# Attention on Trainium2: eight GpSimd row copies per batch, one behind each of eight heads

## The reference, cut to what matters

```
q, k, v = heads(h @ Wq + bq), heads(h @ Wk + bk), heads(h @ Wv + bv)     # [16, 16, 512, 16]
scores  = q k^T + rel_q + rel_k          # rel_*: products with the table of distances
probs   = softmax(scores / sqrt(16))
ctx     = probs v
```

## Time and profile before

| | us |
|---|---|
| median of three runs | 3165.08 |
| the profiled execution's own time | 3169.93 |
| its span, first to last instruction | 3168.1 |
| busy over the whole span: TensorE matmuls | 2673.8 |
| busy: VectorE | 2019.4 |
| busy: ScalarE | 1617.7 |
| busy: GpSimd | 1785.3 |

### The profile page before, as it was taken

The page is one execution under the profiler, slowest core; times in us unless marked ns, Lnnn a source line. Parts: engine busy times, 40 slices in busy tenths (PEclk is TensorE's granted clock), DMA queues, the critical chain, the costliest instruction groups (busy, mean ns, idle before and its releaser), DMA issues. The chain is left out here.

```text
span 3168.1 us, 51305 instructions
## 1 busy us (share of the span) xinstructions
PE 2673.8 (84%) x18316; PEld 1921.7 (61%) x18316; DVE 2019.4 (64%) x5579; ACT 1617.7 (51%) x2037; POOL 1785.3 (56%) x1486
## 2 busy tenths in 40 slices
PE   4676287978988888858999999999999959999998
PEld 2344187877877878755666666666666635554454
DVE  4665255655755666645666666666666658888885
ACT  2343164545544555526777777777777712222221
POOL 2333123333233233228888889988888825655555
PEclk7888667677776777768999999999999979999999
DMA  3999979999999999999999999999999532222110
GB/s 98 222 216 218 187 267 336 365 329 369 361 355 360 349 353 358 342 326 314 286 292 288 288 294 300 289 279 294 294 292 306 184 138 77 70 92 76 70 51 22
DMA packets 499917, 792.66 MB, mean 250 GB/s; under 512 B 236568, under 2 KB 266592, under 8 KB 465616
## 3 DMA queue, kind: packets, MB, share of 16 engines
q1 hardware_dynamic: 440528, 647.27, 61.4%
q10 hardware_dynamic: 46592, 100.68, 13.7%
q0 software_dynamic: 12544, 41.43, 4.5%
HBM read 449.17 MB, written 340.05 MB: 249 GB/s over the span
## 5 line engine op out<-in xcount | busy, mean ns | idle before, releaser
L1054 DVE CUSTOM_DVE_ANT_1 t_neg<-t_ps,t_r 128x512 f32<-128x512 f32 x1024 | 677.8, 686 | 355.2 <-issue 355.0
L733 DVE TENSOR_TENSOR d_r<-d_pq,d_r 128x1024 f32<-128x1024 f32 x512 | 620.7, 1224 | 436.0 <-PE d_pq L660 300.1
L853 POOL TENSOR_SCALAR t_neg<-t_neg,t_low 128x512 f32<-128x512 f32 x512 | 793.0, 1563 | 105.8 <-DVE t_low L1054 100.0
L708 ACT ACTIVATE d_r<-d_pk 128x1024 f32<-128x1024 f32 x512 | 519.4, 1028 | 518.0 <-PE d_pk L673 460.9
L975 PE MATMUL t_pt<-t_ident,t_neg 128*128 128x128 f32 x4096 | 627.5, 276 | 53.9 <-POOL t_neg L853 49.7
L1101 ACT ACTIVATE t_eT<-t_pt 128x1024 f32<-128x1024 f32 x512 | 524.6, 1025 | 258.3 <-PE t_pt L975 251.8
L975 PEld LDWEIGHTS t_pt<-t_ident,t_neg 128*128 128x128 f32 x4096 | 503.1, 142 | 178.2 <-POOL t_neg L853 86.0
L660 PE MATMUL d_pq<-d_win,d_q 96*128 96x128 bf16 x4096 | 502.5, 288 | 103.2 <-POOL d_q L612 76.2
L612 POOL COPY d_q<-d_q 32x4096 f32<-32x4096 f32 x64 | 236.1, 3689 | 602.2 <-DMA d_q<-q_chunks_scratch 602.2
L673 PE MATMUL d_pk<-d_win,d_k 96*128 96x128 bf16 x4096 | 478.5, 276 | 100.2 <-POOL d_k L612 59.2
L660 PEld LDWEIGHTS d_pq<-d_win,d_q 96*128 96x128 bf16 x4096 | 440.4, 189 | 135.7 <-POOL d_q L612 83.5
(11 more groups left out here) (145 smaller groups left out, 2525.0 us busy)
## 6 DMA issues: line engine op xcount, KB each, us to landing
r_scratch<-d_r SPq DMA_DIRECT2D x256, 1024.0 KB, 8.4
t_r<-r_scratch SPq DMA_DIRECT2D x1024, 256.0 KB, 7.9
d_q<-q_chunks_scratch ACTq DMA_DIRECT2D x64, 512.0 KB, 8.6
d_q<-q_chunks_scratch ACTq DMA_DIRECT2D x128, 256.0 KB, 11.6
q_chunks_scratch<-a_part SPq DMA_DIRECT2D x96, 128.0 KB, 3.8
q_rows_scratch<-a_part SPq DMA_DIRECT2D x96, 128.0 KB, 2.5
k_chunks_scratch<-a_part SPq DMA_DIRECT2D x96, 128.0 KB, 3.5
a_x<-in_x POOLq DMA_DIRECT2D x16, 512.0 KB, 5.6
```

Source lines behind the costliest of these rows:

```text
L708: nc.scalar.activation(r[lc % 2][:, :, n * KR:(n + 1) * KR], pk[n % 2][:].rearrange("p r l -> p l r"), ACT.Copy).then_inc(k_out, 1)
L733: nc.vector.tensor_tensor(part, pq[n % 2][:], part, ALU.add).then_inc(q_added, 1)
L853: nc.gpsimd.tensor_scalar(neg[:, j % RING, t, :], neg[:, j % RING, t, :], low[:, j % RING, t:t + 1], None, ALU.subtract).then_inc(pool_sub, 1)
L1054: nc.vector.tensor_tensor_reduce(out=neg[:, j % RING, t, :].rearrange("p (c r) -> p c r", r=TB), in0=p_s[t % 2][:].rearrange("p (c r) -> p ...
```

## The change

The eight copies of a batch are given out singly. `COPIES` names eight heads, 10, 11, 12, 14, 15, 16, 18 and 19, counted from the start of the batch before; so 16, 18 and 19 are heads 0, 2 and 3 of the batch that uses the rows. Copy m is of the query rows of group m // 2 for even m and of its key rows for odd m. Only the first copy of a batch waits for the loaded rows. Each copy has its own wait for GpSimd's last subtraction and for its own end. TensorE's waits are as before. Batch 0 is as before.

```diff
-        COPIES = (10, 11, 12, 14)
+        COPIES = (10, 11, 12, 14, 15, 16, 18, 19)
...
-                def copy_rows(b, i, subtracted):
+                def copy_rows(b, m, subtracted):
+                    i = m // 2
                     heads = slice(b % 2 * H + GH * i, b % 2 * H + GH * (i + 1))
-                    pool.wait_ge(batch_loaded, BATCH * (b + 1))
+                    if m == 0:
+                        pool.wait_ge(batch_loaded, BATCH * (b + 1))
                     later(pool, pool_sub, subtracted)
...
+                    if m % 2 == 0:
+                        nc.gpsimd.tensor_copy(qa[T_Q_COPY: ...], qa[0:T_PAIR, ...]).then_inc(batch_copied, 1)
+                    else:
+                        nc.gpsimd.tensor_copy(kb[T_K_COPY: ...], kb[0:T_PAIR, ...]).then_inc(batch_copied, 1)
+                    pool.wait_ge(batch_copied, 2 * BG * b + m + 1)
 
                 pool.wait_ge(ident_done, 1)
-                for i in range(BG):
-                    copy_rows(0, i, 0)
+                for m in range(2 * BG):
+                    copy_rows(0, m, 0)
                 for n in range(NH + GH + 2):
                     head(n // U, n % U)
-                    b, j = n // H + 1, n % H
-                    if b < nb and j in COPIES:
-                        copy_rows(b, COPIES.index(j), 2 * (n + 1))
+                    for m, place in enumerate(COPIES):
+                        b = (n - place) // H + 1
+                        if (n - place) % H == 0 and 1 <= b < nb:
+                            copy_rows(b, m, 2 * (n + 1))
```

More of the change, by code:

```diff
@@ L879, in head @@
                         copy_v(step, j // GH)
-                def copy_rows(b, i, subtracted):
+                def copy_rows(b, m, subtracted):
+                    i = m // 2
                     heads = slice(b % 2 * H + GH * i, b % 2 * H + GH * (i + 1))
-                    pool.wait_ge(batch_loaded, BATCH * (b + 1))
+                    if m == 0:
+                        pool.wait_ge(batch_loaded, BATCH * (b + 1))
                     later(pool, pool_sub, subtracted)
[L886 to L893, removed]
+                    if m % 2 == 0:
+                        nc.gpsimd.tensor_copy(
+                            qa[T_Q_COPY:T_Q_COPY + T_PAIR, 0, heads, :].rearrange("r h w -> r (h w)").bitcast(F32),
+                            qa[0:T_PAIR, 0, heads, :].rearrange("r h w -> r (h w)").bitcast(F32)).then_inc(batch_copied, 1)
+                    else:
+                        nc.gpsimd.tensor_copy(
+                            kb[T_K_COPY:T_K_COPY + T_PAIR, :, heads, :].rearrange("r c h w -> r c (h w)").bitcast(F32),
+                            kb[0:T_PAIR, :, heads, :].rearrange("r c h w -> r c (h w)").bitcast(F32)).then_inc(batch_copied, 1)
+                    pool.wait_ge(batch_copied, 2 * BG * b + m + 1)
```

## The result

| | before | changed |
|---|---|---|
| median, us | 3165.14 (4 runs, 3159.57 to 3175.03) | 3128.81 (4 runs, 3128.04 to 3137.11) |
| ratio to before, 95% interval | | 0.9888 (0.9858 to 0.9918) |
| profiled execution: own time, span | 3169.93, 3168.1 | 3137.11, 3135.3 |
| first add of attention, from the span's start | 1432.77 | 1439.99 |
| length of a batch in attention | 68.72 | 66.07 |

The changed kernel is 36.3 us faster in the median; 3131 were forecast, and the time lies inside the range of 3116 to 3148. Beside later experiments the same kernel gave ratios of 0.9873 (0.985 to 0.9897) and 0.9846 (0.9822 to 0.987).

A forecast was written before the change was run, and what follows sets the result against it. GpSimd, late behind the copies, was taken to make TensorE wait, 4.25 us per attention batch. With 1.9 us left, 15 batches x 2.3 = 34.5 us took the median from 3165.08 to 3130.6, forecast as 3131; range 3116 to 3148.

The forecast's parts named there:

- What bounds the kernel now: Attention stage: TensorE waits for GpSimd, late behind row copies of heads 10, 11, 12, 14; 4.25 us lost per batch.
- The allowances: Subtraction-pair lateness before TensorE waits: heads like 12 (A) 0.09 us, 13 (B) 1.86, 14 (C) 0.45, 15 (D) 1.44.
- the reserves: GpSimd's possible lateness still starting a subtraction pair on time: B none, C 0.92 us, D 0.53, A 1.39.
- The walk: Head-by-head sum of GpSimd's lateness and TensorE's shift over a batch: 4.18 us lost before, 1.9 with the change.
- A single copy: GpSimd's hold between subtractions by one row copy: 1.25 us; 1.18 would leave 1.4 us per batch, 1.30 would leave 2.3.
- 1.9 us per batch stay: Attention batch with the change: 1.9 us still lost instead of 4.25, paid at heads 16 and 20.
- The sum: 15 batches x 2.3 us = 34.5 us off the kernel; median from 3165.08 to 3130.6 us.
- Rival 1: Attention's loads of distances come late: four batches lose up to 1.5 us, 6 us in all; chance 0.08.
- Rival 2: Copies at heads 16 and 20 cost their full 1.25 us, loss about 4 again: 3165 us; chance 0.05.
- rival 3: Copies fully hidden in attention, the full 63.8 us gained: 3101 us; chance 0.03.
- What would show it: Signs: copies about 1.25 us, batch about 66.4 us, TensorE's waits for GpSimd under half, at heads 16 and 20.
- Rival 4: Copies at new places held up beside VectorE's adds, 0.69 us each: 3213 us; chance 0.04.

The follow-up runs named there:

- e1: Changed kernel without the row copies from batch 2 on: 3112.11 us, ratio to before 0.9833, batch 64.50 us.
- e2: Changed kernel with single copies behind heads 10, 13, 15, 17, 19, 21, 23, 25: 3115.54 us, ratio to before 0.9834, batch 64.49 us.
- e8: The changed kernel itself, run again on another chip: 3131.2 us, ratio to before 0.9873, batch 66.07 us.
- e10: The changed kernel itself, run again on one chip with e9: 3119.86 us, ratio to before 0.9846.
- e4: Changed kernel with single copies behind heads 10, 11, 14, 15, 18, 19, 22, 23: 3118.08 us, ratio to before 0.984, batch 64.80 us.
- e9: The kernel of e2 again, on one chip with e10: 3118.1 us, ratio to before 0.9835.
- e6: Changed kernel with pairs of copies behind heads 11, 15, 19, 23: 3136.08 us, ratio to before 0.9896, batch 66.20 us.
- e5: Changed kernel with pairs of copies behind heads 12, 16, 20, 24: 3148.12 us, ratio to before 0.9938, batch 67.60 us.
- e7: Changed kernel without row loads and row copies from batch 2 on: 3106.9 us, ratio to before 0.98, batch 64.50 us.

## Why the prediction was right, point by point

- *"What bounds the kernel now": GpSimd, late behind the copies, 4.25 us per batch, 63.8 in all.* Right. Without copies a batch takes 64.50 us (e1), with copies that never make GpSimd late 64.49 (e2).
- *The allowances (0.09 in A, 1.86 in B, 0.45 in C, 1.44 in D) and the reserves.* Right in what they forecast for other places: pairs behind A 67.60 us (66.5 to 68.2 expected), behind D 66.20 (66.1). Too strict for pairs behind C: 64.53 where up to 66.0 was allowed for. The walk gives time back only in A heads; TensorE gives back more.
- *A single copy: 1.25 us, bounds 1.18 and 1.30.* 1.19 measured for seven of the eight, 1.26 for the first. The difference is the wait for loaded rows, which the change leaves out for seven copies; the prediction put leaving it out at nothing because it was already fulfilled, and it is worth 0.07 us each time. So the change is two edits in one, and no run separates them. By the walk (an estimate), leaving out the waits alone, with the pairs where they were, is worth 0.2 us a batch; with all eight copies at 1.26 the new places would leave 2.0 us instead of 1.5.
- *1.9 us per batch stay, paid at A16 and A20, with 0.46 shifted at C14.* 1.59 stay (66.07 - 64.48), with waits at A12, C14, A16, C18 and A20; those of A12 (0.23 and 0.48, for a forecast shift of 0.49) come back but for 0.06 (0.08 forecast). The walk with the measured copies, 1.26 for the first and 1.19 for the others, gives 1.5, and 0.76 behind A16 where the pattern has slid by 0.82; most of the forecast's error is that term.
- *The sum: 15 x 2.3 = 34.5 us.* 15 x 2.65 = 39.8, and 39.5 between the attention stages of the two profiles, but 36.3 between the medians. The forecast of 3131 was 2 us off, closer than its terms deserve: an under-estimate of 5 us met a difference of chance outside attention. The profiled execution reached attention 7.2 us later, and of the others no trace tells. That the two nearly cancelled is luck.
- *Rival 1, distances that come late.* In the changed kernel it cost one batch of the profile 0.5 us (66.54), and the smallest reserve was 0.15 us, for 1.0 before. But that is not a fixed property of the kernel: in e8, the same kernel, one batch is 1.5 us too long (67.58), and in e10, again the same, the reserve never falls under 3.6 us from the second batch on. Why executions differ so is open. The mechanism is real, and the 6 us it was given are more than any of the three profiles lost. It takes back part of the next step (e1 to e4, e9).
- *Rival 2, nothing gained; rival 3, all hidden.* Both out: 66.07 us against 68.7 and 64.5.
- *What would show it.* A batch of 66.07 us, groups without copies at 16.12 (heads 8 to 11), the clock at 0.99 and copies of even length came as forecast. Two signs did not. The waits of turns for GpSimd are 69% of what they were (59.6 of 86.0 us), not under half, and heads 12 to 14 are not nearly free of them: A12 waits 0.71 us, C14 0.23. A wait is not yet lost time, and the walk counts only what is lost.
- *Sums and readings.* The term of 1.18 us leaves 1.3 per batch by the walk, not 1.4. The lower end of 3116 is 3 us under what its terms give (3123 less 4). The covers of TensorE's waits for copies are 4 heads for group 0 (behind head 11, wanted at 15), 5 for group 1, then 7 and 8, not "seven or eight"; they sufficed, no turn or score of the changed kernel waits for a row copy within attention. The larger reserves of the batches before go from 2.5 to 5.8 us, not to 6.4.
- *Rival 4, copies held up beside VectorE.* Out. The copies' own rows of the changed kernel (ns min/median/max) are those of the earlier trace rows:

```profile
L889 POOL COPY t_qa<-t_qa x64: 1028/1032/1037, 1437.1 to 2444.4; 32x1024 f32<-32x1024 f32 x64
L893 POOL COPY t_kb<-t_kb x64: 1029/1034/1037, 1438.2 to 2448.7; 32x1024 f32<-32x1024 f32 x64
```

## What to carry to other kernels

Work on an engine that is not the bound is free up to the idle time that passes between it and the next thing someone waits for; so read the allowance of every consumer position from the timeline, and put each piece of side work where the allowance is largest, one allowance apart from the next. Check such a walk by running it over the kernel as it is: here it gave 4.18 us for a measured 4.25. Then it forecast the changed placement within 0.3 us a batch and e2, e4 and e6 within 0.3, had e5 inside a range of 1.7, and allowed up to 1.5 too much for pairs behind C. Price the waits that an edit takes away too, also those that are already fulfilled. And look at the reserve of the stage's loads before shortening it: with 1 us left in the worst batch, waits for a DMA queue took back 4 us (e2) and 14 us (e9) of the 24 that the last 1.59 us a batch would have given.

## What was not expected of the hardware

A load of 256 KB, one of a head's four, took 3.8 us in the median and 6.3 at most to land where no row loads ran beside it (e7, 1900 to 2400 us), and 7.8 and up to 19.4 where they did (e9, same stretch), though the mean rate there was only 301 GB/s against 278. Which of the row loads does this (those of queries have rows of 16 KB each, those of keys of 2 KB) was not tried.

GpSimd's wait for loaded rows, already fulfilled, took 0.07 us at the first copy of every batch (0.13 us between subtraction and copy); copies without it began 0.06 us behind their subtraction.
